# x turned to token rows by VectorE block transposes and a DRAM scratch instead of TensorE transposes, in a Mamba-2 layer with a LoRA feed-forward

## The reference

```python
proj = layernorm(x) @ in_proj_w.T
gate, xBC, dt = split(proj)                     # 8192, 8192 + 2 * 8 * 128, 128 columns
xBC = silu(causal_conv4(xBC) + conv_b)          # per channel, 4 taps over tokens
hs, Bm, Cm = split(xBC)                         # hs: tokens x 128 heads x 64
dt = softplus(dt + dt_bias); cum = cumsum(dt * A)      # within a chunk
scores = einsum('bcihn,bcjhn->bcijh', Cc, Bc) * Ldec * dtc
y_intra = einsum('bcijh,bcjhp->bcihp', scores, xc)
states = einsum('bcjh,bcjhn,bcjhp->bchpn', dtc * dlast, Bc, xc)
y = y_intra + einsum('bcihn,bchpn->bcihp', Cc * exp(cum), prev) + D * hs
g = group_rmsnorm(y * silu(gate)) * norm_w
x = x + g @ out_w.T
x = x + ffn(layernorm(x))       # silu(h1) * h3, each with a LoRA term, then w2 with its own
```

## Time and profile before

| | us |
|---|---|
| median of 3 runs | 1737.63 (1737.61 to 1738.30) |
| span of the profiled execution, first to last instruction | 1737.2 |
| what lies around the span, against the median | 0.4 |
| TensorE busy | 1724.5 (99%) |
| VectorE busy | 1221.0 (70%) |
| ScalarE busy | 1192.8 (69%) |
| GpSimd busy | 1182.1 (68%) |

### The profile page before, as it was taken

One profiled execution on the slowest core, in us unless ns is written; L12 is line 12 of the kernel. 1 busy time (PEld: TensorE's weight loads), 2 busy tenths in 40 slices (PEclk: granted clock), 3 DMA queues, 4 the chain that ended last, 5 costly groups with the idle time before them and its releaser, 6 DMA issues.

```text
span 1737.2 us, 27735 instructions
## 1 busy us (share of the span) xinstructions
PE 1724.5 (99%) x9925; PEld 1436.9 (83%) x9925; DVE 1221.0 (70%) x2154; ACT 1192.8 (69%) x2232; POOL 1182.1 (68%) x1058
## 2 busy tenths in 40 slices
PE   9999999999999999999999999999999999999999
PEld 7788888888888888888888888888888888787887
DVE  8886778768785769676875878586867688663323
ACT  6887677767867677767776777768777777663421
POOL 5586768677777668676867687766867686774510
PEclk9999999999999999999999999999999999999999
DMA  5534435343543443443534354345343353444201
GB/s 192 171 107 116 125 116 169 109 119 105 162 128 114 121 146 112 121 116 112 174 115 115 97 162 128 114 122 151 114 118 113 110 174 101 118 114 134 80 15 49
DMA packets 122056, 211.63 MB, mean 122 GB/s; under 512 B 24256, under 2 KB 28992, under 8 KB 121920
## 3 DMA queue, kind: packets, MB, share of 16 engines
q1 hardware_dynamic: 121920, 209.87, 41.7%
HBM read 205.09 MB, written 4.72 MB: 121 GB/s over the span
## 4 chain that ended last, share of the span: by engine, by line
PE 97%; DVE 1%; DMA 1%; POOL 0%; ACT 0%; issue 0%; POOLq 0%
PE bank L1712 19%; PE bank L1714 18%; PE bank L1713 18%; PE bank L1788 7%; PE bank L1846 7%; PE bank L1836 7%; PE bank L1829 7%; PE bank L1803 5%; PE bank L1762 2%; PE bank L2091 1%; PE bank L2092 1%; PE bank L2093 1%; PE bank L1862 1%; PE bank L1772 1%; PE bank L1953 1%; DMA w_raw<-in_wp 0%
## 5 line engine op out<-in xcount | busy, mean ns | idle before, releaser
L704 POOL TENSOR_TENSOR w_l<-w_raw,w_h 128x512 fp32r<-128x512 f32 x288 | 379.6, 1321 | 341.2 <-ACT w_h L900 341.2
L1712 PE MATMUL bank<-x_h,w_h 128*128 128x512 f32 (+1 forms) x1328 | 527.0, 397 | 3.9 <-DVE x_ch L1385 2.3
L1714 PE MATMUL bank<-x_h,w_l 128*128 128x512 f32 (+1 forms) x1328 | 519.7, 391 | 0.0
L1713 PE MATMUL bank<-x_l,w_h 128*128 128x512 f32 (+1 forms) x1328 | 518.1, 390 | 0.0
L1385 DVE SCALAR_TENSOR_TENSOR x_ch<-bank,par,x_ch 128x511 f32<-128x511 f32 (+2 forms) x384 | 287.2, 749 | 80.3 <-ACT x_ch L918 71.2
L953 ACT ACTIVATE decay<-decay,cols 128x128 f32<-128x128 f32 x1024 | 318.2, 390 | 3.7 <-DMA cdec<-cdec_scratch 1.6
L1712 PEld LDWEIGHTS bank<-x_h,w_h 128*128 128x128 f32 (+1 forms) x1328 | 249.5, 188 | 55.1 <-issue 3.1
L1714 PEld LDWEIGHTS bank<-x_h,w_l 128*128 128x128 f32 (+1 forms) x1328 | 249.2, 188 | 54.6
L1713 PEld LDWEIGHTS bank<-x_l,w_h 128*128 128x128 f32 (+1 forms) x1328 | 249.7, 188 | 51.1
L1415 DVE TENSOR_TENSOR decay<-decay,bank 128x512 f32<-128x512 f32 x256 | 171.3, 683 | 107.1 <-ACT decay L953 107.1
L918 ACT ACTIVATE x_ch<-bank,par 128x512 f32<-128x512 f32 x128 | 99.0, 774 | 185.6 <-PE bank L1714 185.5
(11 more groups left out here) (161 smaller groups left out, 2760.0 us busy)
## 6 DMA issues: line engine op xcount, KB each, us to landing
w_raw<-in_wp SPq DMA_DIRECT2D x288, 256.0 KB, 3.0
decay<-cum_scratch SPq DMA_DIRECT2D x256, 256.0 KB, 4.1
ec<-ecum_scratch SPq DMA_DIRECT2D x96, 256.0 KB, 6.2
ow_raw<-in_ow SPq DMA_DIRECT2D x64, 256.0 KB, 4.8
w_raw<-in_w SPq DMA_DIRECT2D x48, 256.0 KB, 2.7
acc<-in_x SPq DMA_DIRECT2D x8, 256.0 KB, 4.5
out<-acc SPq DMA_DIRECT2D x8, 256.0 KB, 2.0
cols<-cols_scratch SPq DMA_DIRECT2D x16, 96.0 KB, 2.7
```

Source lines behind the costliest of these rows:

```text
L704: pool.tensor_tensor(w_l[:, s, :], w_raw[:, s, :], w_h[:, s, :].bitcast(F32), ALU.subtract).then_inc(wl_ready, 1)
L1712: pe.matmul(dst, wh, xh, start=(opens and k == 0), stop=False)
L1713: pe.matmul(dst, wh, xl, start=False, stop=False)
L1714: last = pe.matmul(dst, wl, xh, start=False, stop=(k == len(terms) - 1 and not more))
```

## The change

`turn_x` leaves TensorE. VectorE transposes all 32x32 blocks of the chunk's x in one instruction, from `x_ch` to `x_sq` (laid over `gT_l`). A 128x128 transpose also needs the blocks themselves moved from partitions to columns, and this is done by writing to DRAM: SP stores `x_sq` in four pieces of 32 partitions (128 KB, runs of 1 KB) to a scratch of two chunks, waits until all four have landed, and fetches the 512 KB back into `xw` with tokens on partitions. `scale_x` then reads `xw` instead of PSUM. GpSimd's `gT_low` waits for the stores, since it writes over `x_sq`, and several waits of TensorE on `xdt_ready` become waits on `state_ready`.

```diff
+            def store_x(g, k):
+                K = g * CHUNKS + k
+                sp.wait_ge(x_turned, K + 1)
+                dst = xt_dram[K % 2].rearrange("(b t) (c f) -> c t b f", b=QUADS, c=QUADS)
+                for q in range(QUADS):
+                    sp.dma_start(dst[q], x_sq[q * SQ:(q + 1) * SQ, :, :, :].rearrange("p b n t -> p b (n t)")).then_inc(x_stored, 16)
+
+            def fetch_x(g, k):
+                K = g * CHUNKS + k
+                sp.wait_ge(x_stored, 16 * QUADS * (K + 1))
+                if some(n_state(g, k)):
+                    sp.wait_ge(st_done, n_state(g, k))
+                sp.dma_start(xw[:, :], xt_dram[K % 2]).then_inc(x_fetched, 16)
...
                         for q in range(QUARTERS):
                             sp.wait_ge(in_done, K * QUARTERS + q + 1)
                             load_decay(gn, kn, q)
+                            if q == 1 and c < SC - 1:
+                                store_x(gn, kn)
+                        if c < SC - 1:
+                            fetch_x(gn, kn)
...
+                    if c == SC - 1:
+                        store_x(gn, kn)
                     for i in tiles[2 if first else 1:-1]:
                         load_next_w(g, last, b, i)
+                    if c == SC - 1:
+                        fetch_x(gn, kn)
...
             def gT_low(g, k):
                 pool.wait_ge(gTh_ready, K + 1)
+                if not (isinstance(g, int) and K == GROUPS * CHUNKS - 1):
+                    pool.wait_ge(x_stored, 16 * QUADS * (K + 2))
...
             def scale_x(g, k):
-                dve.wait_ge(tx_done, K + 1)
+                dve.wait_ge(x_fetched, 16 * (K + 1))
...
-                for h in range(2):
-                    last = dve.tensor_tensor(per_head(xdt[:, half(h)]), per_head(xt[h][:, :]),
-                                             spread(cols[:, b, DT, c, h * 8:h * 8 + 8], HDIM), ALU.mult)
+                for a in range(2):
+                    by = dts[:, a, :].unsqueeze(2).unsqueeze(3).broadcast_to([P, CT, QUADS // 2, SQ])
+                    last = dve.tensor_tensor(xd[:, a, :, :, :], xs[:, a, :, :, :], by, ALU.mult)
...
+            def turn_x(g, k):
+                if c == 0:
+                    dve.wait_ge(silu_done, conv_no(2 * g + b, CONV_TILES))
+                if some(K) and some(K - 1):
+                    dve.wait_ge(out_done, 2 * (K - 1))
+                dve.transpose(x_sq.rearrange("p b n t -> p n b t"), x_ch[:, b, :, tok(c)]).then_inc(x_turned, 1)
...
                     if k != 1:
                         fade(g, k)
+                    if c < SC - 1:
+                        turn_x(gn, kn)
                     add_skip(g, k)
+                    if c == SC - 1:
+                        turn_x(gn, kn)
```

More of the change, by code:

```diff
@@ L163, in build @@
         sgT_r = sc("sgT_r", [P, BATCH, CT, SEQ], F32R)
[L164 to L165 removed]
+        x_ch = sc("x_ch", [P, BATCH, CT, SEQ])
         ow_h = sc("ow_h", [P, CT, HID], F32R)
@@ L182, in build @@
         y_r = sc("y_r", [P, CT, P], F32R)
-        gT_h, gT_l = sc("gT_h", [P, CT, P], F32R), sc("gT_l", [P, CT, P], F32R)
+        gT_h = sc("gT_h", [P, CT, P], F32R)
+        x_sq = under("x_sq", [P, QUADS, CT, SQ])
+        gT_l = sc("gT_l", [P, CT, P], F32R)
         b_tok_h, b_tok_l = sc("b_tok_h", [P, P], F32R), sc("b_tok_l", [P, P], F32R)
@@ L255, in build @@
         bank = [ctx.enter_context(nc.psum_tensor(f"bank{i}", [P, 512], F32)) for i in range(8)]
-        xt_r = [b.bitcast(F32R) for b in bank[2:4]]
         pj, xt, yb, cbb, ob = bank[0:2], bank[2:4], bank[4:6], bank[6], bank[7]
@@ L1720, in norm_transpose @@
                     pe.wait_ge(x_l_ready, c - 3)
-                if k == 1 and c in (2, SC, SC + 1):
-                    pe.wait_ge(xdt_ready, (GROUPS - 1) * CHUNKS + (SC if c == 2 else c + 2) + 1)
+                if k == 1 and c == 2:
+                    pe.wait_ge(x_l_ready, CHUNKS + 1)
+                if k == 1 and c in (SC, SC + 1):
+                    pe.wait_ge(state_ready, n_state(GROUPS - 1, c + 2))
                 if k == 1 and c == SC - 1:
@@ L1750, in project @@
                                                 for q in range(KT)]).then_inc(pj_done, 1)
-            def turn_x(g, k):
-                K, b, c = g * CHUNKS + k, k // SC, k % SC
-                if c == 0:
-                    pe.wait_ge(silu_done, conv_no(2 * g + b, CONV_TILES))
-                if K == MIDDLE + 1:
-                    pe.wait_ge(x_l_ready, CHUNKS + 2)
-                if some(K):
-                    pe.wait_ge(xdt_ready, K)
-                    pe.wait_ge(state_ready, n_state(g, k))
-                for n in range(CT):
-                    last = pe.transpose(xt_r[n // 4][:, tok(n % 4)], x_chr[:, b, n, tok(c)], ident_r[:, :])
-                last.then_inc(tx_done, 1)
             def match(g, k):
@@ L1813, in new_state @@
                 pe.wait_ge(xw_l_ready, n_state(g, k) + 1)
-                pe.wait_ge(xdt_ready, K + 1)
+                if some(n_state(g, k)):
+                    pe.wait_ge(state_ready, n_state(g, k))
                 if g == GROUPS - 1 and k in (SC, CHUNKS - 2):
```

30 lines of the change are left out of this document (20 added, 10 removed).

## The result

| | us |
|---|---|
| before, median of 4 runs | 1737.97 (1737.61 to 1738.37) |
| changed kernel, median of 4 runs | 1947.07 (1935.15 to 1958.86) |
| ratio | 1.12, 95% interval 1.1151 to 1.1248 |
| profiled execution, span | 1941.6, before 1737.2 |

The forecast was 1820 with a range up to 1890. The direction was right, the size was not: the cost of the change is 209 us, and my sum had 82. The changed kernel's own four runs spread over 24 us, so a version of it that comes within about 9 us of its median isn't told apart from it.

What follows compares the result with a forecast made beforehand. TensorE, 99% busy, was taken to bound the kernel, any new wait paid in full. -40.3 (transposes) + 68.6 (ends of halves) + 37 (group starts) + 8.7 + 2 + 6 = +82 on 1737.2: about 1820 us, range 1780 to 1890.

Steps and rivals of the forecast that it cites:

- Removed transposes: TensorE, every chunk: the eight transposes hold its queue for 0.63 us, so 64 chunks save 40.3 us.
- The ends of halves: Chunks 3 and 7 of a group: TensorE waits 4.9 us for accumulate at 14 places, 68.6 us (bounds 3.5 and 7.1 each).
- Ordinary chunks: Some forty chunks: accumulate ends 2.1 us before TensorE needs the bank, so nothing is lost, even at the upper bounds.
- the chain's upper bound: From the last store's issue to fetched data: 6.8 us taken, upper bound 9.0.
- My 20 us: Estimate that the skill page's rule for landings (2.3 and 3.2 us) would make the total about 20 us lower.
- First chunks of a group: First two chunks, groups 1 to 7: late taps cost 3.9 us, late gating 1.4 more; 37 us together (bounds 27 and 52).
- Start, and the last half group: Chunk 0 loses 8.7 us, group 0's second chunk 2, the last half group's four handovers 1.5 each, 6 together.
- The clock, a rival: Products after TensorE's new waits run at the lower clock: up to 77 us, half of that gives 1858; chance 0.14.
- the prediction's own signs: Profile after: 14 waits for accumulate of 3.5 to 7 us, no wait in ordinary chunks, granted clock 1.00, among others.
- The block transpose: VectorE, one per chunk: 1.3 us (bounds 1.1 and 2.2), free in ordinary chunks, on top in a group's second chunk.
- The multiply, put at nothing: VectorE's multiply by dt stays two instructions of 512 elements, left at 1.3 to 1.4 us together.
- the long chain: Rival: stores and fetch take 3 us more; ordinary chunks lose 0.9 each, ends and group starts 3 each: 1920; chance 0.08.

Runs made afterwards that it cites:

- e14: e1 without the block transposes, leaving only TensorE's transposes removed and the multiply reading SBUF; output not the reference's; 1712.1 us (0.9847).
- e1: Changed kernel without its stores, fetch and all waits for them; the multiply reads x_ch, output not the reference's; 1728.3 us (0.9937).
- e11: Changed kernel with all waits, but stores of 8 KB and a fetch of 32 KB; the multiply reads x_ch, output not the reference's; 1827.9 us (1.0512).
- e3: Changed kernel with products that nobody reads put on TensorE where it waits for accumulate; 1925.6 us (1.1068).
- e10: Changed kernel with the fetch ahead of the third and fourth decay load in SP's queue, except in last chunks of a half; 1943.9 us (1.118).
- e9: Changed kernel with the block transpose ahead of the fade of the state in VectorE's list, except in last chunks of a half; 1936.4 us (1.1137).
- e15: Changed kernel with all transfers and waits, but the multiply reads the PSUM banks instead of the fetched data; output not the reference's; 1930.0 us (1.1101).
- e8: Changed kernel with the slot's first weight load ahead of the stores and the second ahead of the fetch (ends of halves: stores between the two); 2027.2 us (1.1652).
- e13: e1 with the multiply reading the PSUM banks instead of x_ch; output not the reference's; 1713.4 us (0.9853).
- e4: Kernel before, keeping TensorE's transposes and multiply from PSUM, with block transpose, stores and fetch added beside; GpSimd waits for stores and fetch; 1814.9 us (1.0427).
- e6: e4 with the same stores, fetches and waits, but a store moves 8 KB and the fetch 32 KB; 1753.2 us (1.0082).
- e12: Changed kernel with accumulate ahead of the multiply, the transpose ahead of the fade, and the fetch ahead of the third and fourth decay load; 1895.1 us (1.091).

## Why the prediction was wrong

The ladder of the medians, each step one thing added:

| kernel | us | step |
|---|---|---|
| before | 1738 | |
| e14, TensorE without its transposes (-41), multiply from SBUF (+15) | 1712 | -26 |
| e1, with the block transpose on VectorE | 1728 | +16 |
| e11, with the chain of waits, nearly empty | 1828 | +100 |
| changed kernel, with all bytes | 1947 | +119 |

The sum fell short by 127 us, 122 in the profiled execution. By the table of places 54 of these lie in ordinary chunks, 37 in the first chunks of groups, 26 at the ends of halves, 5 at the start and in the last half group.

**Removed transposes, right.** 0.70 us per chunk where nothing else waits, against 0.63.

**The ends of halves, right in the wait.** 68 us of idle time against 68.6, 4.9 each as forecast. That the size fits to a tenth is partly luck, since two errors cancel: on the mean of the 14 the last store landed 10.2 us after the inside product where the sum had 9.4, and the fetch took 3.5 where it had 4.2. Here the fetch is the last thing issued for a while: in the half shown it was issued at 923.26 and the multiply began at 926.52. The clock comes on top, 29 us by the granted clock; e3 gives back 1.4 each.

**Ordinary chunks, the step that failed.** "The margin is 2.1 us, so nothing is lost, and at the upper bounds still nothing": 64 us. The last clause didn't even follow from the sum: the chain's upper bound is 2.2 us longer than what was taken, a tenth over the margin, and the block transpose had an upper bound too. And the two landings came out at their upper bound on the mean (9.1 us against 9.0), with a later start ahead of them and a longer multiply behind. The steps, over all 36 ordinary chunks:

| step, us | in the sum | measured, mean (least to most) |
|---|---|---|
| last store issued, after the inside product | 2.9 | 3.7 (3.0 to 4.7) |
| last store's landing | 2.6 | 3.0 (2.3 to 3.8) |
| fetch's landing | 4.2 | 6.0 (4.5 to 8.0) |
| fetch is there, after the inside product | 9.7 | 12.8 (11.2 to 14.8) |
| two multiplies | 1.4 | 1.8 (1.3 to 3.3) |

The multiply ends 3.5 us later than in the sum, over a margin of 2.1. No step by itself is over the margin, so none is the cause alone. In the chunk shown:

```profile
889.70 2.05 SPq L501 DMA_DIRECT2D xt_scratch<-x_sq  x4
893.62 0.32 SPq L509 DMA_DIRECT2D xw<-xt_scratch  x1
```

The largest, the landing of the fetch (5.7 at the median of all 64 places, over my upper bound of 5.6 even there), was priced from the wrong rows. The issue list of the kernel before has two that I left out of the earlier trace rows, the loads that stand in SP's list right behind the fetch's place, and a second load of the fetch's size:

```profile
ec<-ecum_scratch SPq DMA_DIRECT2D x96, 256.0 KB, 6.2
hidden_0b<-in_lb SPq DMA_DIRECT2D x1, 516.0 KB, 7.3
```

A chunk's loads come in one burst, and the fetch stands in the middle of it. The same stretch before, from 2 us after the inside product on:

```profile
881.20:885.20 4.00, 4.00 (x19) 3.33 (x20) 3.49 (x11) 0.18 (x1) 2.55 (x3) 1.00 0.87 300
885.20:889.20 4.00, 4.00 (x34) 3.74 (x33) 2.92 (x5) 3.36 (x5) 2.08 (x3) 1.00 0.84 207
889.20:893.20 4.00, 4.00 (x19) 3.27 (x19) 2.58 (x5) 1.88 (x3) 3.80 (x4) 1.00 0.24 55
```

and after:

```profile
888.60:892.60 4.00, 4.00 (x19) 3.33 (x20) 4.00 (x11) 2.47 (x3) 1.45 (x2) 1.00 0.84 231
892.60:896.60 4.00, 3.96 (x27) 3.24 (x26) 3.72 (x7) 3.36 (x5) 2.90 (x5) 1.00 0.90 246
896.60:900.60 4.00, 4.00 (x20) 3.29 (x19) 2.11 (x1) 0.78 (x1) 3.56 (x3) 1.00 0.99 282
```

The DMA share (the last column but one) was already above 0.8 for eight microseconds; the new megabyte makes it twelve. The second step is the start of the chain: VectorE, which stood idle for the fetch in the chunk before, reaches fade and transpose late. The third is the multiply itself, up to 1.9 us longer for two. Each was taken away by itself. The earlier fetch (e10) ends all waits for accumulate in ordinary chunks, with others in their place; the earlier transpose (e9) and the multiply from PSUM (e15) take 13 and 16 us off their 41; without the bytes (e11) they lose nothing.

The Trainium skill's rule for a landing (page "DMA: Bandwidth & Descriptors", section "Anatomy of one DMA — SWDGE (gpsimd) path") is 2.0 us plus bytes over 436 GB/s, 3.2 us for the fetch. It was fitted to transfers that GpSimd issues, and here SP issues them. The runs show 3.4 with little ahead of the fetch (e10, and the ends of halves), 6.0 in the burst. My 20 us for what that rule would take off the sum were too few: 1.3 us of chain in 14 ends, 7 group starts and the first chunk are 29. The Trainium skill, same page, section "Queues, rings and completion order", says that each of the DMA engines takes its descriptors in ring order. The traces agree: 512 KB of decay issued behind the fetch instead of ahead of it took its landing from 5.7 to 3.4 us (e10), and a weight load issued ahead of the stores took theirs from 3.0 to 3.7 (e8, medians of all).

**First chunks of a group, half of it.** 64 us against 27. In the group shown by the timelines the fetch landed 15.3 us after the inside product where the sum had 12.1 (840.1, less 828.0 for the inside product of the kernel before):

```profile
939.48 2.64 SPq L501 DMA_DIRECT2D xt_scratch<-x_sq  x4
945.14 0.32 SPq L509 DMA_DIRECT2D xw<-xt_scratch  x1
...
951.18 1.32 DVE L1444 TENSOR_TENSOR xdt<-xw,cols 128x512 f32<-128x512 f32 x2 [7.64 <-DMA xw<-xt_scratch]
```

The stores were issued when the sum had them (the last 5.1 us after the inside product, 5.2 in the sum). It is the landings again: 4.2 us for the last store where I took 2.6, and 6.0 for the fetch, with output weights and decays ahead of both. I had not named the block transpose's wait for the last output product of the half before (46.5 us in 14 places), but it ends 0.1 us after the inside product begins and delayed nothing that the sum had earlier. VectorE then works without a gap, so all of it reaches the taps. The clock took 24 us more, which filling the waits didn't give back.

**Start, and the last half group, near.** 12 and 10 us against 10.7 and 6, within the bounds.

**The clock, a rival that came true beside the others.** It had 0.14 and 38 us; e3 gives 21. It isn't an alternative to the other cases but comes on top of the waits, here in all 14 ends and all 7 first chunks, and belonged into the sum. The full clock and the ordinary chunks without a wait were two of the prediction's own signs, and both failed.

**The block transpose, right in size.** 1.24 us (1.3 taken). It costs 16 us (e14 to e1), where I had about 10, in the second chunks of a group alone. **The multiply, put at nothing.** I left it at 1.3 to 1.4 us because its size stayed; its operand went from PSUM to SBUF, and that costs 15 us (e13).

**What I had not seen.** The weights (e4 to e6). A weight load that was issued 3.6 us after the inside product began now follows at 8.5, and lands behind fetch and ec. In the changed kernel this is partly hidden, since TensorE stands anyway. ScalarE's waits for weights are also long in e10 and e12 (186 and 126 us), but no run shows what they cost there.

The rival nearest to the truth was the long chain (1920), with the right mechanism for ordinary chunks (0.9 us each, measured 1.8) and a chance of 0.08. That was too low: its condition, a chain 3 us longer, followed from the bytes in the burst, which the windows of the kernel before show. No version that computes the layer beats the kernel before; even without any transfer the change would be worth 0.6% (e1), or 1.5% without the block transpose too (e14). Versions that move fewer bytes for the same result, or use another queue than SP's, were not tried.

## What to carry to other kernels

A transfer put into a burst costs three times: its own landing grows with what stands ahead of it, what stands behind it lands later, and an in-order engine that waits for it starts its next link late. So take the landing from rows of the same moment of the chunk (here the `ec` loads), with the DMA share beside it, not from the median of the kernel, and check the slack of every load that is issued behind it. When an operand moves from PSUM to SBUF, look at what GpSimd does at that time.

## What the runs showed of the hardware

- A block transpose of 128x1024 four-byte elements takes 1.21 to 1.25 us on VectorE, in all 64 cases.
- A VectorE multiply of 128x512 with both operands in SBUF took up to 2.9 us instead of 0.69 beside a GpSimd instruction that reads SBUF (e1, and 2.6 in the changed kernel); with one operand in PSUM it stayed at 0.69 (e4, e13, e15).
- A store of 8 KB landed in 2.4 us at the median, a load of 32 KB in 2.7 (e11); at 128 and 512 KB they took 3.0 and 5.7 at the median of all places. The 512 KB load took 4.5 to 8.0 in the burst of an ordinary chunk and 3.2 to 4.3 at the ends of halves.
- A wait of TensorE of 4.5 us was followed by 3.5 us at a granted clock of 0.52. In ordinary chunks, with waits of 0.7 to 2.8 us, the clock stayed full in 33 of 36.
